# A Fourier layer's mode mixing with kx innermost, another order of PSUM evacuations, and split sums

## What is computed

```python
def _fourier_layer(v, W1, W2):            # v: (64, 32, 64, 64)
    x_ft = rfft2(v)
    out1 = einsum('bixy,ioxy->boxy', x_ft[:, :, :12, :12], W1)
    out2 = einsum('bixy,ioxy->boxy', x_ft[:, :, -12:, :12], W2)
    ...                                   # both into a zero spectrum
    return irfft2(out_ft)
for i in range(4):
    x1 = _fourier_layer(v, W1, W2)
    x2 = einsum('bcxy,cd->bdxy', v, w_w[i]) + w_b[i]
    v = batch_norm(x1 + x2)               # mean and variance over images and pixels
    if i < 3: v = relu(v)
```

## Time and profile before

| | us |
|---|---|
| median of 3 runs | 1580.74 |
| lowest and highest run | 1577.38, 1595.98 |
| the profiled execution | 1593.06 |
| its span, first to last instruction | 1591.2 |
| PE, DVE, ACT, POOL busy | 1226.5, 890.3, 526.9, 277.4 |
| mean granted clock of TensorE | 0.875 of 2.4 GHz |

### The profile page before, as it was taken

How to read it: one execution, slowest core, us unless ns; L and a number is a source line. 1 busy time by engine, 2 the same in 40 slices (tenths; PEclk the granted TensorE clock), 3 DMA queues, 4 the chain that set the end, 5 groups by cost and what they waited for, 6 DMA issues and landing times.

```text
span 1591.2 us, 40180 instructions
## 1 busy us (share of the span) xinstructions
PE 1226.5 (77%) x18183; PEld 695.7 (44%) x18183; DVE 890.3 (56%) x945; ACT 526.9 (33%) x778; POOL 277.4 (17%) x381
## 2 busy tenths in 40 slices
PE   3567599999957679888995676998889756953587
PEld 3333255555532235545553333554555443223562
DVE  6445367767735537655764643665656622027745
ACT  1123235444433314444342331443434333020140
POOL 5532300120213220202020313020202031200000
PEclk9778779999977879999998877998989978985688
DMA  5437788897524789999981368999899253951001
GB/s 140 100 87 192 189 192 189 218 223 189 135 51 120 193 207 312 285 328 304 312 256 32 107 179 192 327 308 300 259 306 286 72 186 118 374 207 45 2 0 27
DMA packets 164675, 300.20 MB, mean 189 GB/s; under 512 B 32776, under 2 KB 111000, under 8 KB 147284
## 3 DMA queue, kind: packets, MB, share of 16 engines
q1 hardware_dynamic: 150042, 261.83, 57.2%
q0 software_dynamic: 14464, 35.81, 8.3%
HBM read 150.22 MB, written 128.48 MB: 175 GB/s over the span
## 4 chain that ended last, share of the span: by engine, by line
PE 60%; DVE 16%; DMA 7%; ACT 7%; issue 6%; SPq 4%; POOL 0%; DVEq 0%; ACTq 0%
PE ps L1437 14%; PE ps L1473 11%; PE ps L1505 6%; PE ps L1493 6%; PE ps L1398 5%; PE ps L1462 3%; PE ps L1377 3%; DVE arena L1732 2%; PE ps L1367 2%; PE ps L1453 2%; DMA maps<-arena 2%; PE ps L1567 2%; ACT arena L1254 1%; SPq L956 1%; DMA arena<-half_inverse 1%
## 5 line engine op out<-in xcount | busy, mean ns | idle before, releaser
L1473 PEld LDWEIGHTS ps<-arena 48*128 48x128 f32 x3072 | 193.2, 199 | 114.5 <-issue 92.3
L1473 PE MATMUL ps<-arena 48*128 48x128 f32 x3072 | 213.5, 291 | 31.8 <-DMA arena<-half_inverse 19.0
L956 POOL DMA_DIRECT2D arena<-arena x162 | 95.7, 599 | 790.3 <-ACT arena L1271 789.6
L1254 ACT ACTIVATE arena<-ps,arena 128x1024 f32<-128x1024 f32 x96 | 112.4, 1203 | 247.5 <-PE ps L1473 206.0
L1263 ACT ACTIVATE ps<-ps 128x1024 f32<-128x1024 f32 x144 | 145.5, 1011 | 110.5 <-PE ps L1437 110.2
L1828 DVE STREAM_TRANSPOSE arena<-ps 128x1024 f32<-128x1024 f32 x96 | 177.1, 1929 | 0.7 <-PE ps L1493 0.5
L1437 PE MATMUL ps<-arena 32*32 32x512 f32 x2944 | 161.9, 625 | 8.3 <-issue 7.2
L1818 DVE STREAM_TRANSPOSE arena<-arena 128x2048 f32<-128x2048 f32 x64 | 144.3, 2293 | 22.8 <-issue 13.0
L1493 PE MATMUL ps<-arena 32*32 32x512 f32 x3072 | 149.1, 602 | 6.0 <-DVE arena L1818 3.4
L1505 PE MATMUL ps<-arena 128*64 128x96 f32 x2304 | 127.9, 264 | 32.7 <-DVE arena L1828 28.6
L1505 PEld LDWEIGHTS ps<-arena 128*64 128x64 f32 x2304 | 108.4, 147 | 90.2 <-issue 51.6
(11 more groups left out here) (305 smaller groups left out, 1408.1 us busy)
## 6 DMA issues: line engine op xcount, KB each, us to landing
half_inverse<-arena SPq DMA_DIRECT2D x144, 256.0 KB, 4.0
arena<-half_inverse SPq DMA_DIRECT2D x96, 384.0 KB, 9.1
maps<-arena SPq DMA_DIRECT2D x112, 256.0 KB, 4.1
maps<-inputs SPq DMA_DIRECT2D x112, 256.0 KB, 6.1
arena<-maps SPq DMA_DIRECT2D x28, 1024.0 KB, 10.3
maps<-arena SPq DMA_DIRECT2D x28, 1024.0 KB, 5.5
inputs<-maps SPq DMA_DIRECT2D x28, 1024.0 KB, 9.0
arena<-in_mode_w POOLq DMA_DIRECT2D x48, 384.0 KB, 4.1
```

Of the source, the lines that this page charges most:

```text
L1254: nc.scalar.activation(half(h_out(l, q), h)[:, 1024 * pair:1024 * pair + 1024], ps[:, 2 * pair:2 * pair + 2, :].rearrange("p b n -> p (b n ...
L1473: last = nc.tensor.matmul(ps[:, b, at:at + 128], gtile[s][rows, 4 * b + 2 * h + n, :], iy[rows, :], start=False, stop=(i >= 2 and n == 1))
```

## The change

- **Layout.** In the first three layers the mixed modes have kx innermost: 24 values of kx and 8 of padding for each image, 32 floats. The mode products therefore write PSUM with a step of 6 floats (24 bytes) where they wrote 64 neighbours; the skip products write neighbours where they wrote with a step of 64 floats. ACT's copy reads PSUM in order, and writes runs of 6 floats. The transposes read neighbours where they read with a step of 64 floats. The fourth layer's `last_modes` keeps its layout, so there ACT's copy writes, and DVE reads, with a step of 64 floats, where both went over neighbours.
- **Evacuations.** Of groups 0 to 17 the even ones go to DVE and the odd ones to ACT, each right behind its own half step in the queues; groups 18 to 23 all go to ACT.
- **Sums.** Each unit's tensor_tensor_reduce of 768 elements becomes two of 384 with a sum each (`sums_ox` has 24 columns, which are added up in `norm_sums`). For unit 0 only what frees the PSUM stays ahead; the other statistics (`first_sums`) come after the first `turn_kx`, ahead of unit 2's sums. In the fourth layer they stand there too.
- **Padding.** POOL zeroes it once a layer, after the first unit's products, and DVE waits for `pads_zero`.

```diff
@@ -892,9 +892,9 @@
                 for turn in range(2):
                     steps.append(("half", u, turn))
                     if 2 * u + turn >= AHEAD and groups:
-                        steps.append(("inverse", groups[0], groups.pop(0) % 2))
+                        steps.append(("inverse", groups.pop(0), 0))
             for n in groups:
-                steps.append(("inverse", n, n % 2))
+                steps.append(("inverse", n, 0))
             return steps + [("sums", 0, 0), ("norm", 0, 0)]
 
 
...
@@ -902,6 +902,17 @@
 
         def inverse_bank(n):
             return 6 if n < LAST_GROUPS else (6, 0, 2)[(n - LAST_GROUPS) % 3]
+
+        def evac_of(l, n):
+
+            own = LAST_GROUPS // 2
+            if n >= LAST_GROUPS:
+                return 0, (own + AHEAD) * l + own + n - LAST_GROUPS + 1
+            return (0, (own + AHEAD) * l + n // 2 + 1) if n % 2 else (1, own * l + n // 2 + 1)
+
+        def wait_group(eng, l, n):
+            who, count = evac_of(l, n)
+            eng.wait_ge(ix_ev[who], count)
 
         def skip_bank(u):
...
@@ -992,8 +1003,8 @@
                         sp.dma_start(dst, first_stage[1][32 * j:32 * j + 32, :, at:at + 144]).then_inc(first_st, 16)
             def store_inverse(l, p, i):
 
-                for g in range(2):
-                    sp.wait_ge(ix_ev[g], mode_of(l, 2 * p + i + 1))
+                for n in range(2):
+                    wait_group(sp, l, 4 * p + 2 * i + n)
                 j = (i + first_half(l)) % 2
                 both = view((A_G, A_P)[p % 2], 4096).rearrange("p (e q n) -> p e q n", e=2, n=128)
                 for e in range(2):
...
@@ -1135,6 +1146,13 @@
                 place_part(pool, l, batch, 1)
 
             for l in range(LAYERS):
+                if l < PASSES:
+                    pool.wait_ge(mix_full, mode_of(l, 0) + 1)
+                    pool.wait_ge(signed, 2 * (KY * l + RING))
+                    for s in range(2):
+                        pads = mixed(l, s).rearrange("p (b x) -> p b x", b=BATCH)[:, :, KX:32]
+                        nc.gpsimd.memset(pads, 0.0).then_inc(pads_zero, 1)
+                    pool.wait_ge(pads_zero, 2 * l + 2)
                 for ky in range(KY):
                     pool.wait_ge(mix_full, mode_of(l, ky | 1) + 1)
                     if ky + RING < KY:
...
@@ -1220,8 +1238,10 @@
                 first_evac(nc.scalar.copy, q).then_inc(spread_ev_0[0], 1)
 
             def mixed_target(l, u):
-                of_two = mixed(l, u // 2)[:, 0:1536] if l < PASSES else last_modes[:, u // 2]
-                return of_two.rearrange("p (m h k b) -> p h m k b", m=2, h=2, b=BATCH)[:, u % 2]
+                if l < PASSES:
+                    return mixed(l, u // 2).rearrange("p (b x) -> p b x", b=BATCH)[:, :, 0:KX]\
+                        .rearrange("p b (m h k) -> p h m b k", m=2, h=2)[:, u % 2]
+                return last_modes[:, u // 2].rearrange("p (m h k b) -> p h m b k", m=2, h=2, b=BATCH)[:, u % 2]
 
             def mix(l):
                 for what, n, part in mix_order(l):
...
                         src = ps[:, 2 * (n % 2):2 * (n % 2) + 2, 0:384]
-                        nc.scalar.copy(mixed_target(l, n), src.rearrange("p h (k b) -> p h k b", b=BATCH))\
+                        nc.scalar.copy(mixed_target(l, n), src.rearrange("p m (b k) -> p m b k", b=BATCH))\
                             .then_inc(mix_ev, 1)
                         act.wait_ge(mix_ev, i + 1)
                         nc.scalar.activation(src, src, ACT.Square, accum_out=sums_oo[:, n:n + 1] if n else unused)\
                             .then_inc(mix_sq, 1)
-                    elif what == "inverse" and part == 0:
+                    elif what == "inverse" and evac_of(l, n)[0] == 0:
                         act.wait_ge(ix_full, group_of(l, n) + 1)
...
@@ -1364,7 +1384,8 @@
                     for e in range(2):
                         for m in range(2):
                             rows = slice(64 * m, 64 * m + 64)
-                            last = nc.tensor.matmul(ps[64 * e:64 * e + 64, 2 * s + m, 64 * k:64 * k + 64],
+                            last = nc.tensor.matmul(ps[64 * e:64 * e + 64, 2 * s + m, 0:384]
+                                                    .rearrange("p (b k) -> p k b", b=BATCH)[:, k],
                                                     ring[(2 * p + e) % RING][rows, 6 * h + k, :],
                                                     modes[rows, :, e, p, 6 * h + k], start=True, stop=True)
                 if turn:
@@ -1374,8 +1395,7 @@
                 for m in range(2):
                     e = (turn + m) % 2
                     rows = slice(64 * m, 64 * m + 64)
-                    last = nc.tensor.matmul(ps[64 * e:64 * e + 64, skip_bank(u) + m, 0:384]
-                                            .rearrange("p (k b) -> p b k", b=BATCH),
+                    last = nc.tensor.matmul(ps[64 * e:64 * e + 64, skip_bank(u) + m, 0:384],
                                             wbd[l][rows, 64 * m:64 * m + 64], modes[rows, :, e, p, 6 * h:6 * h + 6],
                                             start=True, stop=True)
...
                 elif n <= LAST_GROUPS:
-                    pe.wait_ge(ix_ev[(n - 1) % 2], mode_of(l, (n - 1) // 2 + 1))
+                    wait_group(pe, l, n - 1)
                 elif n < LAST_GROUPS + 3:
                     pe.wait_ge(mix_sq, mode_of(l, KY - 2 + n - LAST_GROUPS - 1) + 1)
                 else:
-                    pe.wait_ge(ix_ev[(n - 3) % 2], mode_of(l, (n - 3) // 2 + 1))
+                    wait_group(pe, l, n - 3)
                 for e in range(2):
                     rows = slice(64 * e, 64 * e + 64)
                     last = nc.tensor.matmul(ps[:, b + e, :], ix[rows, :], kxin(l, p)[rows, 512 * c:512 * c + 512],
...
-                return of_two.rearrange("p (m h k b) -> p h m k b", m=2, h=2, b=BATCH)[:, u % 2]
+                if l < PASSES:
+                    return mixed(l, u // 2).rearrange("p (b x) -> p b x", b=BATCH)[:, :, 0:KX]\
+                        .rearrange("p b (m h k) -> p h m b k", m=2, h=2)[:, u % 2]
+                return last_modes[:, u // 2].rearrange("p (m h k b) -> p h m b k", m=2, h=2, b=BATCH)[:, u % 2]
+
+            def scratch(l):
+                tile = spectra if l < PASSES else turned
+                return (tile[:, at:at + 768].rearrange("p (m b k) -> p m b k", m=2, b=BATCH) for at in (0, 768))
+
+            def pairs_of(l, u, o):
+
+                own, held = scratch(l)
+                link(ttr(out=held[0:64, 0], in0=o[0:64, 0], in1=o[0:64, 1], scale=1.0, scalar=0.0, op0=ALU.mult,
+                         op1=ALU.add, accum_out=pair_sums[0:64, u:u + 1]))
 
             def mode_sums(l, u):
                 i = mode_of(l, u)
                 o = of_mode(l, u)
+                b = skip_bank(u)
                 dve.wait_ge(mix_ev, i + 1)
                 dve.wait_ge(x2_full, i + 1)
-                tile = spectra if l < PASSES else turned
-                own, held = (tile[:, at:at + 768].rearrange("p (m k b) -> p m k b", m=2, b=BATCH) for at in (0, 768))
                 if u == 0:
 
-                    link(tt(first_row, o[:, 0, 0, :], ps[:, 4, 0:64], ALU.add))
-                    link(nc.vector.reduce_sum(m_sum, first_row, AX.X))
-                    link(tt(cols2[:, 1:2], m_sum, real, ALU.mult))
-                    link(ts(t2, m_sum, 1.0 / BATCH, None, ALU.mult))
-                    link(ts(junk_row, first_row, t2, None, ALU.subtract))
-                    link(ttr(out=first_row, in0=junk_row, in1=junk_row, scale=1.0, scalar=0.0, op0=ALU.mult,
-                             op1=ALU.add, accum_out=zero_sum))
-                    if l:
-                        link(nc.vector.tensor_copy(junk_row, ps[:, 4, 0:64]))
-                        link(ttr(out=first_row, in0=junk_row, in1=junk_row, scale=1.0, scalar=0.0, op0=ALU.mult,
-                                 op1=ALU.add, accum_out=skip_sum))
+                    own, held = scratch(l)
+                    skip = ps[:, b, 0:384].rearrange("p (b k) -> p k b", b=BATCH)[:, 0]
                     link(nc.vector.tensor_copy(own, o))
-                    link(nc.vector.memset(own[0:64, 0, 0, :], 0.0))
-                    link(ttr(out=held, in0=own, in1=own, scale=1.0, scalar=0.0, op0=ALU.mult, op1=ALU.add,
-                             accum_out=sums_oo[:, 0:1]))
+                    link(nc.vector.tensor_copy(junk_row, skip))
+                    link(tt(first_row, own[:, 0, :, 0], junk_row, ALU.add))
+                    link(nc.vector.memset(own[0:64, 0, :, 0], 0.0))
                     o = own
-                if u < 2:
-
-                    link(ttr(out=held[0:64, 0], in0=o[0:64, 0], in1=o[0:64, 1], scale=1.0, scalar=0.0, op0=ALU.mult,
-                             op1=ALU.add, accum_out=pair_sums[0:64, u:u + 1]))
-                b = skip_bank(u)
-                x2 = ps[:, b:b + 2, 0:384].rearrange("p m (k b) -> p m k b", b=BATCH)
```

(37 more changed lines are left out.)

7 lines of the change are left out of this document (3 added, 4 removed).

## The result

| | before | after |
|---|---|---|
| median of the runs, us | 1587.72 (4 runs, 1577.38 to 1595.98) | 1519.16 (4 runs, 1511.27 to 1524.36) |
| profiled execution, span, us | 1591.2 | 1513.6 |
| mean granted clock | 0.875 | 0.891 |

The account below looks back on a forecast made before the run. Bound by a loop of waits in the mix stages, then by the DMA engines: 56 us gained in three stages, 12.5 lost in the fourth, - 43.5 in all, so 1537 us from a median of 1580.74; range 1511 to 1569.

Parts of the forecast that it names:

- the loop of waits: Mix stages: PE idles 3.70 us before an inverse group, awaiting an evacuation behind DVE's transposes; the change leaves no wait.
- better than that: Rival: DMA engines fill to 1.0 and ACT's copy doesn't mind the step; - 68 + 5.5, so 1518 us; chance 0.15.
- Start of a stage: Each of the first three mix stages: stores begin at 489.5 us, 5.4 us before the 494.9 of the kernel before.
- The limit of the transfers: First three mix stages: DMA engines set the pace, 64.4 us from first store to eleventh landing; 18.7 us gained a stage.
- The transfers don't pack: Rival: the DMA share in the mix stages rises only to 0.78, gaining 16.5 us less 12.5; 1577 us; chance 0.16.
- The step on SP: Mix stage: SP's 44 issues are 34 us of work, 48 at 1.1 us each, so SP isn't the limit.
- Transposes: First three mix stages: reading neighbours, a transpose takes 1.2 us for 1024 elements; the pair falls from 3.6 to 2.4.
- sums: Splitting each unit's sum in two adds 0.1 us a unit, 0.14 as bound; hidden in the first three layers.
- runs: ACT's copy writing runs of 24 bytes costs nothing extra; at the other end 0.5 us on the copy, still hidden.
- PSUM: Mode products writing PSUM with a step of 24 bytes: priced at 0.
- two of the rivals: Products slowed by their PSUM step: twice as long, 1564 us, chance 0.07; three times, 1616 us, chance 0.04.
- The fourth layer: Fourth mix stage: steps in ACT's copy and DVE's sums plus the split cost 1.28 us a unit; 12.5 us lost.

Follow-up runs that it names:

- e5: The changed kernel with only 64 of 768 floats a row loaded from the seventh mode-weight load on, so old weights are used; 1516.91 us, ratio 0.953.

## Why the prediction was right, and where it was off

The direction, the place and the loop of waits held; the size was too small by more than a third (43.5 us of 68.6), because the limit named for what is left, the DMA engines, was not the one that holds. That the measured 1519.16 us lie beside the 1518 of the rival "better than that" is luck: it had 68 us won in three stages and 5.5 lost in the fourth, and 83.2 and 16.2 were measured. (Its 5.5 also leaves out the 1 us at the start: 0.6 x 9 + 1 is 6.4.)

**The loop of waits: right.** PE's idle time before the inverse groups is gone, the groups take 1.13 us instead of 2.08, and each half of the change alone leaves a part of the wait (1.16 and 2.46 us). "No wait is left on PE" is what the timeline of after shows; how much there is to spare it doesn't show.

**Start of a stage: right.** The first store was forecast 22.6 us after the stage's start (489.5 - 466.91), and went at 22.6 (459.74 - 437.13). Unit 11's products end at 497.2, 60.1 us after it; forecast 60.7. The 22nd group is out at 505.0, 67.9 after it; forecast about 69.

**The limit of the transfers: the step that failed.** From the first store to the landing of the eleventh I forecast 64.4 us; it took 515.56 - 459.74 = 55.8. That is 8.6 us a stage, 26 in all. It has three parts, and the first was to be had beforehand. I took the DMA work of a pair from the window 500 to 562, 11.0 us, and multiplied by 5.5 pairs. The window of the kernel before that covers the interval itself says less:

```profile
494.90:572.60 77.70, 56.60 (x514) 24.16 (x515) 39.60 (x60) 24.25 (x36) 25.41 (x26) 0.81 0.73 190
```

77.7 x 0.73 = 56.7 us of work, not 60.5. Eight weight loads and 33 of the store DMAs lie in the window from 500 to 562; in the whole interval there are 44 store DMAs and still eight loads. The 1.5 pairs that I added have stores only, and I charged them three loads at 1.2 us each. At 0.94 the interval's own work gives 60.3 us: 4.1 of the 8.6. Then the work itself fell to 55.9 x 0.97 = 54.2 (2.7 us at 0.94), for the same stores and one weight load more; why, no run shows. And the share rose to 0.97, above the 0.94 of the earlier trace rows (1.8 us). I had taken that as its height, from the stage's last 7 us, which hold the load and the twelfth store; "no window of this stage is over 0.94" holds of the windows in the earlier trace rows, not of the stage. The kernel before has

```profile
550.00:555.00 5.00, 2.00 (x20) 0.57 (x12) 3.72 (x4) 2.15 (x4) 4.14 (x5) 1.00 0.97 258
```

The 55.8 us lie below the 60.5 that the prediction gave as the transfers' least, so its rival "better than that" was too long here as well. "The transfers don't pack", with 0.16, is refuted: 1.00 in the middle of the stage.

**Also off: what is the limit.** "The DMA engines, not PE, set the pace" rested on 11.0 against 10.2. It is 10.0 against 10.0, PE has no pause in 32 us, and e5 shows that taking DMA work away frees almost nothing. The eleventh store lands 10.5 us after the 22nd evacuation (78.4 - 67.9), not 18 us after it (553.9 - 536), as forecast. The step on SP put its work at 34 us, 48 with 1.1 us an issue, from a median of 0.774; it is 46. A median over a stage with gaps was no price for one without; the mean in the full stage is 1.05. "SP isn't the limit" held, by 3 to 9 us.

**Transposes, sums, runs, padding, PSUM: right.** 1.221 us for a forecast 1.2; + 0.11 us for the split, forecast 0.1; ACT's copy in runs of six has a median of 0.807 us in the second stage, before 0.805. A POOL zeroing takes 0.52 us, at the low end of 0.5 to 1. The products' median is 285 ns with the step of 24 bytes and was 285 without, and the skips' is 498 ns with a step and without. The Trainium skill (PSUM — Partial Sum Buffer, "Specifications (TRN2)") says that a pattern that is not contiguous slows matmuls significantly; by that rule two of the rivals had the products at two and three times. This kernel's rows, all of fp32, don't agree with it: neither step costs a matmul anything.

**The fourth layer: right in kind, 3.7 us short.** 12.5 us lost were forecast, 16.2 measured. ACT's scattering copy was the unknown, forecast 1.48 us from a DVE row, measured 1.52; the sums were + 0.5, forecast + 0.5; the start + 1.2, forecast about 1. Most of what is missing is the clock. PE's timeline in the fourth stage of the kernel after:

```profile
1211.75 0.90 PE L1398 MATMUL ps<-arena 64*64 64x384 f32 x2 [1.48 <-DVE arena L1736]
...
1232.27 0.91 PE L1398 MATMUL ps<-arena 64*64 64x384 f32 x2 [2.15 <-DVE arena L1736]
...
1234.13 0.83 PE L1398 MATMUL ps<-arena 64*64 64x384 f32 x2
...
1237.72 0.54 PE L1398 MATMUL ps<-arena 64*64 64x384 f32 x2 [1.47 <-DVE arena L1736]
...
1238.88 0.51 PE L1398 MATMUL ps<-arena 64*64 64x384 f32 x2
...
1242.52 0.91 PE L1398 MATMUL ps<-arena 64*64 64x384 f32 x2 [2.15 <-DVE arena L1736]
```

From 1217 us on the units go by turns: after 2.15 us of idle time the skips take 0.91 us, after 1.47 they take 0.54. The spacing goes by turns with them, 5.47 and 4.80 us. The granted clock, in windows of one unit from 1222 us on, is 0.70, 0.99, 0.70, 0.98: of the two levels (1.2 and 2.4 GHz) the slow units have the lower for much of their time. From 1211 to 1252 it is 0.83, where 1300 to 1332 of the kernel before had 0.99. As I read it, a slow unit ends late, which shortens the next idle time, and the next unit is fast again; but the unit at 1211.75 is slow after 1.48 us of idle time, so the idle time just before it is not all that decides, and no run here varies it by itself. By turns a unit takes 5.13 us in the mean for the 4.79 forecast (3.51 + 1.28); over the nine units of the sum that is 3.1 of the 3.7 us. I had costed a longer loop by what was added to it, and not asked what its longer idle time does to the engine in it.

## What to carry to other kernels

Read the work of a shared resource from the very interval that it is to bound, counting what is in it; a rate from the middle, multiplied by the number of steps, charges the end with transfers that it doesn't have. When a wait goes, expect the next limits to stand close together, and take the best share that a resource reaches in a few windows as a lower bound of what it can do, not as its height; and ask which engine has no pause: a share of 1.00 on the DMA engines did not make them the limit. Test the parts of a change alone: here the order of evacuations by itself was worth nearly the whole. And a layout that pays in three stages can cost in the one that hides nothing: the same kernel with the old layout in the fourth layer, and with small work put behind what starts the stores, gives another 25 us (93.2 us below the kernel before that ran beside it, for 68.6).

## What the runs showed of the hardware

- ScalarE's copy out of PSUM of 768 elements takes 0.80 us into neighbours, 0.81 into runs of 24 bytes, and 1.52 us with a step of 256 bytes, 0.94 ns an element more. VectorE's sum over 384 takes 0.81 us reading so, 0.56 without the step.
- A matmul took the same time whether it wrote PSUM with a step of 4 or of 24 bytes (285 ns, 64 columns), and of 4 or of 256 bytes (498 ns, 384 columns).
- The 16 DMA engines were full through 52 us (share 1.00, 279 GB/s) while stores, of 64 partitions each, and weight loads ran together. Moving a fifth less (224 GB/s for 285, share 0.90) left the stages within 0.7 to 2.8 us.
- An issue on SP took 0.57 us at the least. From one to the next it was 1.05 us in the mean for a 256 KB store in the full stage, 0.95 with less other traffic (e5_small_weights), and 0.73 for one of half the size.
- In a closed loop TensorE went by turns between its two levels: 0.54 and 0.91 us for the same two matmuls, at a mean granted clock of 0.83.
